# A scan kernel with y accumulated by channels, the softplus halved between banks, and twice as many states whose input term TensorE makes

## What is computed

```
uc = conv1d(x Win_u, 4 taps) + convb;  u = silu(uc);  z = x Win_z
dtr, Bm, Cm = split(u Wx)                 # 8, 16 and 16 columns
dt = softplus(dtr Wdt + bdt);  A = -exp(Alog)
h[t,n] = exp(dt[t] A[n]) * h[t-1,n] + dt[t] u[t] Bm[t,n]     # 16 states n, 256 channels
y[t] = sum_n h[t,n] Cm[t,n] + u[t] D
out = (y * silu(z)) Wout
```

## Time and profile before

| | |
|---|---|
| median of 3 runs | 1725.72 us |
| profiled execution, its own time | 1706.65 us |
| profiled span | 1704.9 us |
| units, start of the first dtu to that of the last | 36.4 to 915.2 us |
| VectorE busy in the span | 1385.4 us (81%) |
| TensorE matmul busy in the span | 1323.4 us (78%) |
| ScalarE, GpSimd busy | 1062.2 us, 1109.9 us |

### The profile page before, as it was taken

How to read it: one execution, slowest core, us unless ns; L and a number is a source line. 1 busy time by engine, 2 the same in 40 slices (tenths; PEclk the granted TensorE clock), 3 DMA queues, 4 the chain that set the end, 5 groups by cost and what they waited for, 6 DMA issues and landing times. The chain is left out here.

```text
span 1704.9 us, 30907 instructions
## 1 busy us (share of the span) xinstructions
PE 1323.4 (78%) x8880; PEld 958.7 (56%) x8880; DVE 1385.4 (81%) x2234; ACT 1062.2 (62%) x1888; POOL 1109.9 (65%) x1244
## 2 busy tenths in 40 slices
PE   4877788787778777877877658888988888888771
PEld 2656566566656665665666433335665556656671
DVE  2999999999999999999999846676778777777432
ACT  6777777776786776777867315565665656556330
POOL 1777777787877777777868814444557566655535
PEclk8989998899889899898998757898999999999886
DMA  5112302320321123023203021134556455564662
GB/s 190 54 59 101 125 1 99 124 99 4 121 99 61 64 99 124 0 99 124 81 19 141 27 89 30 50 125 134 175 152 200 149 173 168 155 198 134 224 221 72
DMA packets 115274, 186.05 MB, mean 109 GB/s; under 512 B 10736, under 2 KB 87536, under 8 KB 110960
## 3 DMA queue, kind: packets, MB, share of 16 engines
q1 hardware_dynamic: 111056, 176.30, 29.9%
q0 software_dynamic: 4096, 8.40, 1.7%
HBM read 153.92 MB, written 26.15 MB: 106 GB/s over the span
## 5 line engine op out<-in xcount | busy, mean ns | idle before, releaser
L882 DVE TENSOR_TENSOR_SCAN wt<-da,dbu 128x512 f32<-128x512 f32 x448 | 527.6, 1204 | 17.4 <-ACT da L722 6.8
L722 ACT ACTIVATE da<-dt,a_neg 128x512 f32<-128x512 f32 x512 | 351.4, 716 | 186.2 <-DVE wt L882 161.4
L1025 POOL TENSOR_TENSOR hc<-wt,qk 128x512 f32<-128x512 f32 x256 | 327.8, 1299 | 97.2 <-DVE wt L882 75.3
L1025 POOL TENSOR_TENSOR hc<-wt,cb 128x512 f32<-128x512 f32 x256 | 326.1, 1294 | 93.0 <-DVE wt L882 87.9
L491 PE MATMUL yp<-ident,hc 128*128 128x128 f32 x2048 | 321.8, 291 | 5.4 <-POOL hc L1025 5.1
L2018 ACT ACTIVATE pt<-scores,lift 128x512 f32<-128x512 f32 x320 | 216.3, 684 | 167.3 <-PE scores L1761 165.8
L491 PEld LDWEIGHTS yp<-ident,hc 128*128 128x128 f32 x2048 | 271.9, 153 | 84.6 <-issue 52.2
L2149 DVE TENSOR_REDUCE mx<-wp 128x1 f32<-128x384 f32 (+3 forms) x352 | 217.9, 635 | 91.3 <-PE wp L1723 86.9
L866 DVE TENSOR_TENSOR dbu<-dtu,bp 128x512 f32<-128x512 f32 x384 | 251.4, 684 | 10.9 <-PE bp L479 1.0
L2496 POOL TENSOR_SCALAR_AFFINE_SELECT pt<-pt 128x256 f32<-128x256 f32 (+1 forms) x320 | 119.0, 375 | 190.1 <-ACT pt L2018 189.0
L402 PE MATMUL wp<-xpad,wu 128*128 128x512 f32 x256 | 132.5, 610 | 11.6 <-DVE wt L897 6.5
(11 more groups left out here) (252 smaller groups left out, 2441.9 us busy)
## 6 DMA issues: line engine op xcount, KB each, us to landing
wt<-ffn_w_e SPq DMA_DIRECT2D x120, 384.0 KB, 4.4
qk<-c_scratch SPq DMA_DIRECT2D x8, 3072.0 KB, 11.6
cb<-c_scratch SPq DMA_DIRECT2D x8, 3072.0 KB, 11.8
qk<-q_scratch SPq DMA_DIRECT2D x96, 96.0 KB
qk<-c_scratch SPq DMA_DIRECT2D x8, 1024.0 KB, 4.7
cb<-c_scratch SPq DMA_DIRECT2D x8, 1024.0 KB, 4.7
xg<-xs_scratch SPq DMA_DIRECT2D x24, 256.0 KB, 3.4
ys_scratch<-ysb SPq DMA_DIRECT2D x24, 256.0 KB, 3.0
```

The source lines that it names most:

```text
L722: nc.scalar.activation(da[:, s % NDA, :], dt[:, h, :], ACT.Exp, scale=a_neg[:, d, h, n:n + 1]).then_inc(da_done, 1)
L882: nc.vector.tensor_tensor_scan(hb[:, s % NHB, :], da[:, s % NDA, :], src, 0.0, ALU.mult, ALU.add).then_inc(scan_done, 1)
L1025: nc.gpsimd.tensor_tensor(hc[:, s % NHC, :], hb[:, s % NHB, :], cb[d][:, s // 2, :], ALU.mult).then_inc(hc_done, 1)
```

## The change

Four things are edited.

1. `pe_y` no longer transposes. It multiplies the identity (stationary) by 512 columns of `hc` (moving), one fp32 matmul per step, so that y is accumulated with channels on the partitions. `dve_yg` then writes `ygt` directly, `pe_ygt` and `act_ygt` are gone, and `pe_z` is written in the same layout.
2. `BY_PE` names eight states of sixteen in place of four. There are four diagonal buffers.
3. The softplus: the bias bdt comes from a row of ones in `xd`; the Relu instruction on ScalarE is gone; VectorE forms max(x, 0) + ln(1 + exp(-|x|)) straight from the PSUM bank, as two instructions of 128x512 in place of one of 128x1024.
4. `pe_bt` and `act_bt` stand earlier (slots 24 and 29 in place of 30 and 31), and the second `pe_dt` waits for `act_bt`.

```diff
-BY_PE = ((2, 4, 12, 14), (2, 4, 6, 14))
+BY_PE = ((2, 3, 5, 6, 8, 10, 12, 14), (2, 3, 5, 6, 8, 10, 12, 14))
-DIAG_AT = ((-1, 5, 18, 20), (-1, 5, 11, 20))
+DIAG_AT = ((-1, 2, 5, 8, 12, 15, 18, 21), (-1, 2, 5, 8, 12, 15, 18, 21))
...
         def pe_dt(pe, b, d, h):
             if h == 0:
                 pe.wait_ge(silu_done, count(silu_done, b, 4 * d + 4))
                 pe.wait_ge(xd_done, count(xd_done, b, 4 * d + 2))
+            else:
+                pe.wait_ge(bt_done, count(bt_done, b, d + 1))
...
             for h in (range(NH2) if s < 0 else (s % 2,)):
                 src = ud[:, h, :] if s < 0 else hc[:, s % NHC, :]
-                for c in range(TC):
-                    last = nc.tensor.matmul(yp[:, c, h * P:(h + 1) * P], src[:, c * P:(c + 1) * P], ident[:, :],
-                                            is_transpose=True, start=(s < 0 and h == 0 and c % 2 == 0),
-                                            stop=(s == STEPS - 1), skip_group_check=True)
+                last = nc.tensor.matmul(yp[:, h, :], ident[:, :], src, start=(s < 0), stop=(s >= STEPS - NH2),
+                                        skip_group_check=True)
             last.then_inc(y_added, 1)
...
-                if tail and s == 7:
-                    pe_ygt(pe, *tail)
...
-                    if s == 30:
-                        pe_bt(pe, *front)
                     if s in (24, 25):
                         pe_dt(pe, *front, s - 24)
+                    if s == 24:
+                        pe_bt(pe, *front)
...
             act.wait_ge(bt_done, count(bt_done, b, d + 1))
-            act.wait_ge(fill_done, count(fill_done, b, N_PE * d + e - 1))
+            act.wait_ge(fill_done, count(fill_done, b, N_PE * d + e - 3))
...
-                nc.scalar.activation(t_abs[:, :], wp[:, 1 - (h ^ d), :], ACT.Abs, bias=bias).then_inc(soft_done, 1)
+                nc.scalar.activation(t_abs[:, :], wp[:, 1 - (h ^ d), :], ACT.Abs).then_inc(soft_done, 1)
             elif k == 1:
-                nc.scalar.activation(t_relu[:, h, :], wp[:, 1 - (h ^ d), :], ACT.Relu, bias=bias).then_inc(soft_done, 1)
...
-            if k == 0:
-                dve.wait_ge(soft_done, count(soft_done, b, 8 * d + 8))
+            if k < NH2:
+                dve.wait_ge(soft_done, count(soft_done, b, 6 * d + 3 * k + 3))
                 dve.wait_ge(da_done, count(da_done, b, STEPS * d))
-                nc.vector.tensor_tensor(dt[:, :, :], t_ln[:, :, :], t_relu[:, :, :], ALU.add).then_inc(dt_done, 1)
+                nc.vector.scalar_tensor_tensor(dt[:, k, :], wp[:, 1 - (k ^ d), :], 0.0, t_ln[:, k, :],
+                                               ALU.max, ALU.add).then_inc(dt_done, 1)
...
-            nc.vector.tensor_tensor(yg[:, :, :], yp[:, :, :], sz[:, d], ALU.mult).then_inc(yg_done, 1)
+            dve.wait_ge(out_ready, count(out_ready, b, 0))
+            out = ygt[:, d]
+            nc.vector.tensor_tensor(out[:, :, ::-1] if d else out, yp, sz[:, d], ALU.mult).then_inc(yg_done, 1)
```

More of the change, by code:

```diff
@@ L75, in is_first @@
     return isinstance(b, int) and b == 0
+ONE_ROW = DT_ROW + DTR
 FIRST_IN = (2, 4)
@@ L145, in part @@
             return a.rearrange(f"p ({names}) -> p {names}", **dict(zip("abcd", shape)))
-        sz = part(NDIR, TC, DI)
-        yg = part(TC, DI)
+        sz = part(NDIR, NH2, SEQ)
         ygt = part(NDIR, NH2, SEQ)
@@ L160, in mamba_phase @@
         eps = shared["wt"][:, taken:taken + TC]
+        taken += TC
+        diag_more = part(2, TC, P)
         q9, k9 = shared["q9"], shared["k9"]
@@ L381, in pe_xt @@
             if not first:
-                pe.wait_ge(ygt_done, count(ygt_done, b - 1, 2))
+                pe.wait_ge(dtt_done, count(dtt_done, b - 1, 4))
             for c in range(TC):
@@ L409, in pe_z @@
             h = k ^ d
-            for c in (2 * h, 2 * h + 1):
-                last = nc.tensor.matmul(wp[:, h, (c % 2) * DI:(c % 2 + 1) * DI],
-                                        xpad[:, d, NTAP - 1 + c * P:NTAP - 1 + (c + 1) * P], win_z[:, d, :],
-                                        start=True, stop=True)
-            last.then_inc(z_ready, 1)
+            nc.tensor.matmul(wp[:, h, :], win_z[:, d, h * P:(h + 1) * P], xpad[:, d, NTAP - 1:NTAP - 1 + SEQ],
+                             start=True, stop=True).then_inc(z_ready, 1)
         def pe_xd(pe, b, d):
@@ L423, in pe_bt @@
         def pe_bt(pe, b, d):
-            pe.wait_ge(soft_done, count(soft_done, b, 8 * d + 8))
             pe.wait_ge(xd_done, count(xd_done, b, 4 * d + 2))
             for c in range(TC):
-                last = nc.tensor.transpose(wp[:, 0, c * P:(c + 1) * P], xd[:, c * P:(c + 1) * P], ident[:, :])
+                last = nc.tensor.transpose(wp[:, d, c * P:(c + 1) * P], xd[:, c * P:(c + 1) * P], ident[:, :])
             last.then_inc(bt_ready, 1)
         def pe_dtt(pe, b, d):
-            pe.wait_ge(dt_done, count(dt_done, b, 2 * d + 2))
-            pe.wait_ge(soft_done, count(soft_done, b, 8 * d + 8))
+            pe.wait_ge(dt_done, count(dt_done, b, 3 * d + 3))
+            pe.wait_ge(soft_done, count(soft_done, b, 6 * d + 6))
             pe.wait_ge(bt_done, count(bt_done, b, d + 1))
@@ L453, in pe_fill @@
             for c in range(TC):
-                last = nc.tensor.matmul(dst[:, c * P:(c + 1) * P], dtt[:, c, h * P:(h + 1) * P], diag[:, (N_PE * d + e) % 2, c, :],
+                last = nc.tensor.matmul(dst[:, c * P:(c + 1) * P], dtt[:, c, h * P:(h + 1) * P], diag_of(d, e)[:, c, :],
                                         start=True, stop=True)
@@ L636, in act_silu_u @@
                 act.wait_ge(xd_ready, count(xd_ready, b, d))
-                act.wait_ge(dt_done, count(dt_done, b, 2 * d))
+                act.wait_ge(dt_done, count(dt_done, b, 3 * d))
                 if d:
@@ L796, in act_unit @@
                         act_diag(act, b, d, e)
-                if tail and s in (14, 15):
-                    act_ygt(act, *tail, s - 14)
                 if front:
@@ L861, in dve_dbu @@
             if s == 0:
-                dve.wait_ge(dt_done, count(dt_done, b, 2 * d + 2))
+                dve.wait_ge(dt_done, count(dt_done, b, 3 * d + 3))
             if h == 0:
@@ L918, in dve_first_rope @@
                 dve.wait_ge(ffn_loaded, 16 * 4)
-                dve.wait_ge(dt_done, count(dt_done, NB - 1, 4))
+                dve.wait_ge(dt_done, count(dt_done, NB - 1, 6))
             if k < 2:
@@ L957, in dve_unit @@
                         dve_first_rope(dve, k)
-                if front and s in (29, 30):
-                    dve_dt(dve, *front, s - 29)
+                if front and s in (28, 29, 30):
+                    dve_dt(dve, *front, s - 28)
         @block.vector
@@ L1101, in act_last @@
         def act_last(act):
-            act_ygt(act, NB - 1, 1, 0)
-            act_ygt(act, NB - 1, 1, 1)
+            act.wait_ge(yg_done, count(yg_done, NB - 1, 2))
         def dve_last(dve, k):
```

91 lines of the change are left out of this document (39 added, 52 removed).

## The result

| | before | after |
|---|---|---|
| median (runs) | 1724.22 us (4 runs, 1713.73 to 1731.79) | 1866.49 us (4 runs, 1863.44 to 1872.6) |
| profiled execution, its own time | 1706.65 us | 1863.44 us |
| first to last dtu, start to start | 878.8 us, 15 units of 58.6 | 1036.0 us, 15 units of 69.07 |
| TensorE, VectorE busy | 1323.4, 1385.4 us | 1592.3, 1314.2 us |

A forecast was written before the change was run, and what follows sets the result against it. TensorE was to become the bound, its list 60.5 us a unit. 10.4 + 52.4 + 1.3 + 3.1 = 67.2 us a unit, 8.6 more, fourteen times, less 7.0, gave 1820 us profiled, 1840 us as median; range 1778 to 1895.

The forecast's parts named there:

- first rival: TensorE bounds, but the waits at a unit's opening and end overlap with it: 62 us a unit, 1767 us; chance 0.13.
- third rival: Slow clock lasting past the opening, or waits on diagonals or bt in each unit: 72 us or more, 1908 us; chance 0.08.
- first unit: The unit from the first dtu to the second, without a tail: gains about 1 us in length.
- fourteen units: The units with front and tail: 67.2 us each, 8.6 us more than before, +120 us together.
- TensorE's prices: Start-to-start costs on TensorE: y as matmul 0.86 us against 0.44 transposed, half an input term 0.89, B 0.22.
- second rival: The y matmul costs no more than the transposes; VectorE stays the bound at about 54 us: 1649 us; chance 0.05.
- Stage B: The rest of TensorE's list after the gating: 60.5 - 8.1 = 52.4 us, none hidden, plus 1.3 us for waits on ScalarE.
- Stage A: From the end of dtu to the end of gating the previous unit's y: 10.4 us, against 9.9 before.
- Stage C: A unit's end: TensorE idles 3.1 us, before 5.2, while VectorE works 5.1 us from the last input term through dtu.
- ScalarE and the early bt at nothing: ScalarE at about 47 us stays behind; the second pe_dt's wait costs nothing, at most 2.15 us.
- VectorE's list "near 54": VectorE's work in a unit after the change: near 54 us, no longer what sets the unit.
- The clock at the opening: If transposes don't count as clock activity, matmuls end the slow stretch sooner: 9.9 us up to the gating, sum 7 us lower.

The follow-up runs named there:

- slot 23: The changed kernel with ScalarE's silu of u and z in its slot 23 in place of 25: 1849.44 us, ratio 1.078 to the kernel before.
- early-B run: The changed kernel with TensorE spreading B of state 1 ahead of dtu's transposes: 1856.26 us, ratio 1.0795 to the kernel before.
- square of four kernels: All with the new dt and early bt, against the kernel before: y by transposes, four or eight states, 0.9972 and 1.032; y by matmuls, 1.0182 and 1.0848.
- two kernels with six states: The whole change but y, six states placed outside the front's and projection's slots or inside them: 1746.56 us (1.0155) and 1777.4 us (1.0336).
- pairs of slot 25 and 23 with transposes: The change without y, ScalarE's silu two slots earlier: four states 0.9972 to 0.9858, six outer 1.0155 to 0.9981, eight 1.032 to 1.0171.
- second experiment: The kernel before with only the eight states added and three diagonal buffers in place of four: 1911.94 us, ratio 1.115.

## Why the prediction was right, and where its sizes were off

The direction, the mechanism and the range held: 1866.49 us against 1840, between 1778 and 1895. A unit of 69.07 us lies inside the forecast's 64 to 71, above the first rival's 62 and below the third's 72. As medians the sum fell short by 26 us. In the profiled executions' own terms, in which it was made, it fell short by 43: 1863.44 against 1820. The difference is that the profiled execution of before was 1.0% under its median, and that of after 0.2%; that the median came out 17 us nearer than the sum is luck. Both traces, divided at the same places (dtu starts at 36.41, 92.33 and 915.16 us before, 34.67, 101.53 and 1070.70 after; the output projection of the last unit starts at 994.92 and 1145.71):

| stretch | predicted | measured |
|---|---|---|
| to the first dtu | -2.6 | -1.7 |
| first unit | +1 | +10.9 |
| fourteen units | +120.4 (8.6 each) | +146.3 (10.45 each) |
| last unit and its gating, to the projection | -5.4 | -4.8 |
| everything behind | 0 | +6.0 |
| sum | +113.4 | +156.7 |

- **TensorE's prices: right.** A y of 0.86 us, an input term of 0.90, with no exception in the stretches read at the full clock. This was the price on which most hung, and it put the second rival out. The count of records, two against one, gave it against a transpose. It doesn't give a price by itself: a bfloat16 matmul leaves one record too and takes 0.22 us, a quarter.
- **TensorE becomes the bound: right.** TensorE is busy 62.5 and 65.4 us in the two units, and the scans wait for L455. Stage B was predicted as 52.4 + 1.3 = 53.7 us; the two stages took 52.1 (391.70 to 443.82) and 55.3 (459.24 to 514.55), 53.7 on average. z waited 0.75 us or less for u where the term had 1.3; the rest of that is other small waits. At slot 23 the unit lost 1.2 us.
- **Stage A: mis-sized.** 10.4 was predicted; it took 12.3 (379.39 to 391.70) and 11.1 us (448.18 to 459.24), 11.7 on average. The clock of the opening was as forecast, granted 0.50, but "nearly all of this was slack" was wrong. Two y at 1.2 GHz made B of state 1 late, and VectorE, which fills this stage, waited 1.32 and 1.30 us for it, and 0.45 us more ahead of the gating in the second unit. By the profile of the early-B run 0.9 us of that is what it costs.
- **Stage C: mis-sized by the same 1.3 us.** 3.1 was predicted, 4.4 measured (443.82 to 448.18). I counted VectorE's chain from TensorE's last input term, as if VectorE were up to date there. It wasn't: it came out of the late scan at 436.80 with 11.4 us of its own work before the end of dtu, and TensorE, which started its last y at 442.96, ran out of work ahead of it.
- **The first unit: mis-sized most for its length.** It was put at +1 because it has no tail. It took 66.9 us against 55.9. TensorE's list is indeed short there, 60.5 - 4.3 - 2.0 = 54.2 us without five y and the projection. The loss is at its opening:

```profile
35.95:47.50 11.55, 8.30 (x34) 7.32 (x35) 8.55 (x10) 11.55 (x28) 6.28 (x5) 0.50 0.47 150
```
```profile
41.60 3.75 PE L455 MATMUL bp<-diag,wt 128*128 128x128 f32 x16 [3.25 <-issue]
```

With no y of an earlier unit to do, TensorE stood 3.25 us ahead of its first input term. By the order of time it waited for ScalarE's second copy of the transposed dtu, which ended at 41.50. The clock stayed at 0.50 for the 11.55 us from TensorE's start, and from 35.95 to 48.88 us TensorE did work that its prices put at 5.5 us (0.88 + 0.22 + 3 x 0.89 + 2 x 0.86). The 7.4 us lost there, the list's 54.2, the 4.3 us of waiting for the next dtu and 0.6 for u come to 66.5. The prediction had this long slow stretch only as a rival (the slow clock "lasts into stage B"), and in every unit, not in the first alone.

- **The last unit and the end: right** within a microsecond. What stands behind the projection, which the change doesn't touch, took 716.0 us against 710.0. That is 0.35% of the kernel and the cause is open; runs of the kernel before differ by more.
- **ScalarE and the early bt at nothing: nearly right.** ScalarE is busy 48.3 and 44.1 us in the two units. The wait on bt that the third rival named came up in every unit (11 times between 150 and 850 us, 29.4 us in all), but was nearly covered. In one unit bt waited 2.71 us for the transposes of xd and held the da of the scan at 436.80, which ended at 436.75. The input term of that scan ended at 436.60 (435.55 + 1.05), so the wait was worth 0.15 us. Where TensorE is less late it could be worth more.
- **dt: right as a price** (0.68 us twice), and worth nothing that can be told as a time (0.9972, 0.9923 to 1.002).
- **VectorE's list "near 54": right as a sum, wrong as a bound.** VectorE is busy 51.9 and 53.5 us. The step that failed is the second rival's, "VectorE stays the bound at about 54 us": with a y of 0.44 and 0.22 us the units took 62.7 and 59.5. Even with a y of 0.22 us the kernel took 1725.66 us where the rival had 1649. It weighed two lists against each other, but the longer list doesn't set a unit in which both engines wait in order.
- **The clock at the opening: stage A didn't shrink.** The stretch at 0.50 (1.2 GHz) lasted about 5.1 us from TensorE's start (448.42 to 453.50), against 5.5 before, and at the neighbouring opening 5.6 us (379.70 to 385.30) against 3.7 (386.39 to 390.10), though two y as real matmuls lie in it now. The Trainium skill (TensorE: Matmul & The Clock Gate, PE-mode transpose) says that transpose mode doesn't count as busy time of TensorE in the same way; working by that rule the prediction had 9.9 us for stage A. The trace has 11.7. Over whole units the granted clock did rise, from 0.91 and 0.93 to 0.95 and 0.96, but TensorE also waits less there, so these runs don't tell the one cause from the other.
- **Two slips in the working.** The start's 2.6 us isn't what its two named savings add up to (two Relu at 0.671 and 0.8 for dt, 2.1; 1.7 measured), and half-way between 1767 and 1795 is 1781, not 1778. Neither changes the outcome.

What is shown and what is only argued: that y's price makes a large part of the loss is shown by the kernels that differ in it, three with eight states and two with four. That the added states cost as well, and that both parts together cost more than the sum of the two, is shown by the square of four kernels. That the place of the input terms counts is shown by the two kernels with six states. That ScalarE's place for u costs time is shown by the pairs of slot 25 and 23 with transposes; that it closes a ring is read from the waits of one trace. That the rest of what eight states cost with slot 23 (61.2 against 57.5 us) is crowding in the slots of the convolution is an argument from the six-state pair, not tried by itself. How much of the second experiment is its three buffers is open.
